# The steps over the row groups written out in full, in place of a loop on the engines

## The reference, cut to what is computed

```
n = layernorm(x)
bias = n @ Wb                                  # (4 heads, 160, 160)
q, k, v = n @ Wq, n @ Wk, n @ Wv               # 160 rows of 160 tokens, 4 heads of 32
attn = softmax(q k^T / sqrt(32) + bias, masked keys at -1e9)
x1 = x + ((attn v) * sigmoid(n @ Wg)) @ Wo
t = layernorm(x1)
p = softmax(t @ router_w + router_b); the best 2 of 8, renormalised
out = x1 + sum over the best 2 of p_e * (t @ expert_w[e] + expert_b[e])
```

## Time and profile before

| | us |
|---|---|
| median of 3 runs | 902.15 (900.57 to 903.08) |
| the profiled execution, its own time | 900.99 |
| span of that execution, first to last instruction | 899.2 |
| PE busy | 818.6 (91%) |
| DVE busy | 778.2 (87%) |
| POOL busy | 645.3 (72%) |
| ACT busy | 501.9 (56%) |

### The profile page before, as it was taken

The page is one execution under the profiler, slowest core; times in us unless marked ns, Lnnn a source line. Parts: engine busy times, 40 slices in busy tenths (PEclk is TensorE's granted clock), DMA queues, the critical chain, the costliest instruction groups (busy, mean ns, idle before and its releaser), DMA issues.

```text
span 899.2 us, 40916 instructions
## 1 busy us (share of the span) xinstructions
PE 818.6 (91%) x15532; PEld 543.4 (60%) x15532; DVE 778.2 (87%) x1818; ACT 501.9 (56%) x1049; POOL 645.3 (72%) x1029
## 2 busy tenths in 40 slices
PE   1999688999999999999999999999999999999643
PEld 1898346666666666666666666666666666666411
DVE  8998445999999999999999999999999999998754
ACT  3886345655655565565655556555565555665310
POOL 6994002587878778787778777777787877888776
PEclk9999999999999999999999999999999999999855
DMA  4563000011111001010010101100010100100000
GB/s 123 193 199 132 30 17 32 25 40 33 47 39 36 29 29 51 29 36 29 29 51 29 36 29 40 41 33 33 29 47 33 36 29 29 51 24 18 24 7 16
DMA packets 32461, 40.82 MB, mean 45 GB/s; under 512 B 6288, under 2 KB 27280, under 8 KB 32400
## 3 DMA queue, kind: packets, MB, share of 16 engines
q1 hardware_dynamic: 31920, 39.95, 13.6%
q10 hardware_dynamic: 480, 0.02, 0.0%
HBM read 13.74 MB, written 6.55 MB: 23 GB/s over the span
## 4 chain that ended last, share of the span: by engine, by line
PE 71%; POOL 10%; DVE 9%; issue 8%; ACT 1%; DVEq 0%; DMA 0%; POOLq 0%; ACTq 0%
PE psS L1117 12%; PE psS L1092 7%; PE psS L1124 5%; PE ps_r L1148 3%; POOL ln_s L375 3%; PE ps_o L1174 3%; PE ps_m L1174 2%; PE psS L1136 2%; PE ps_o L1177 2%; PE ps_m L1177 2%; PE psS L1097 2%; POOL xn L378 2%; PE ps_o L1008 2%; DVE prod L943 2%; POOL add L428 1%
## 5 line engine op out<-in xcount | busy, mean ns | idle before, releaser
L825 DVE TENSOR_REDUCE negm<-psS 128x12 f16<-128x1920 f32 x80 | 145.3, 1816 | 19.5 <-PE psS L1102 17.7
L428 POOL TENSOR_TENSOR add<-prod 128x256 f32<-128x256 f32 x160 | 116.1, 726 | 1.0 <-DVE prod L943 0.9
L433 POOL TENSOR_TENSOR add<-add 128x128 f32<-128x128 f32 x200 | 91.2, 456 | 5.0 <-issue 0.2
L375 POOL TENSOR_TENSOR ln_s<-ln_s,half 128x5 f32<-128x5 f32 (+1 forms) x60 | 86.2, 1437 | 8.0 <-DVE ln_s L737 7.3
L545 ACT ACTIVATE pt_a<-psS 128x1280 f32<-128x1280 f32 x40 | 49.5, 1238 | 71.1 <-PE psS L1126 71.1
L416 POOL TENSOR_TENSOR og_lo<-og,og_hi 128x320 f16<-128x320 f32 x80 | 63.3, 793 | 32.5 <-ACT og_hi L582 32.5
L394 POOL TENSOR_TENSOR xc<-x,ln_s 128x320 f32<-128x320 f32 x40 | 28.9, 722 | 79.0 <-DVE ln_s L874 79.0
L545 ACT ACTIVATE pt_b<-psS 128x1920 f32<-128x1920 f32 x40 | 70.8, 1771 | 17.0 <-PE psS L1136 16.9
L1117 PE MATMUL psS<-bt_hi,ident 128*128 128x320 f16 (+1 forms) x320 | 67.8, 334 | 8.7 <-issue 5.5
L435 POOL TENSOR_TENSOR ymix<-add 128x64 f32<-128x64 f32 x200 | 64.3, 321 | 15.7
L1092 PE MATMUL psS<-bm,ident 128*128 128x480 f16 (+1 forms) x320 | 68.4, 337 | 1.2 <-ACT pt_a L545 1.1
(11 more groups left out here) (287 smaller groups left out, 2950.4 us busy)
## 6 DMA issues: line engine op xcount, KB each, us to landing
xin<-in_x SPq DMA_DIRECT2D x20, 320.0 KB, 2.9
xs_all<-xs_pair SPq DMA_DIRECT2D x20, 320.0 KB, 2.5
xs_q<-xs_all SPq DMA_DIRECT2D x40, 160.0 KB, 2.1
xs_v<-xs_all SPq DMA_DIRECT2D x40, 160.0 KB, 2.1
xin<-in_x SPq DMA_DIRECT2D x40, 160.0 KB, 2.2
out<-res SPq DMA_DIRECT2D x40, 160.0 KB, 1.8
w_raw<-in_expert_w SPq DMA_DIRECT2D x2, 128.0 KB
eb_raw<-in_expert_b SPq DMA_DIRECT2D x15, 2.0 KB
```

The lines of the kernel that those rows point to most:

```text
L375: pool.tensor_tensor(ln_s[a][:, 3, 0:w], ln_s[a][:, 2, 0:w], half[:, 0:w], ALU.pow).then_inc(own, 1)
L428: pool.tensor_tensor(add1[t % 2][:], prod_of(t)[:, 0:4, :], prod_of(t)[:, 4:8, :], ALU.add).then_inc(mix_step[t], 1)
L433: pool.tensor_tensor(add2[t % 2][:], add1[t % 2][:, 0:2, :], add1[t % 2][:, 2:4, :], ALU.add).then_inc(mix_step[t], 1)
L825: dve.tensor_reduce(negm[c][:, :, 0:slots], psS[:, :, 0:slots * N].rearrange("i h (s j) -> i h s j", s=slots), AX.X, ALU.max, negate=True) ...
```

## The change

`run_steps` no longer calls `pairs_loop`: all 46 steps, -2 to 43, are written out on all five engines, with n as a plain number. PE's table of who frees which PSUM bank, which had to be set by hand at the entry of the loop body and behind it, is no longer set, since the written-out order gives the same entries. `N_CONST` becomes 23, so the wait at L753 is for all 23 constants in place of 22, and the one at L880 for 25 in place of 24. The order of the work within a step is untouched on every engine. The loops of the first stage stay.

```
-        N_MEMSET, N_CONST = 18, 22
+        N_MEMSET, N_CONST = 18, 23
...
-        FIRST, LOOP, LOOP_END, LAST = -2, 7, GROUPS - 3, GROUPS + 4
+        FIRST, LAST = -2, GROUPS + 4

         def run_steps(eng, step):

-            for n in range(FIRST, LOOP):
-                step(n, n % 2)
-            pairs_loop(eng, step, LOOP, LOOP_END)
-            for n in range(LOOP_END, LAST):
+            for n in range(FIRST, LAST):
                 step(n, n % 2)
...
             def step(n, a):
                 b = 1 - a
-                if not isinstance(n, int) or n == LOOP_END:
-
-                    last[id(psS)] = max_done[1], n + 1
-                    last[id(ps_r)] = qkl_done[1][1], n + 2
-                    last[id(ps_m)] = prod_done[3], n - 3
-                    last[id(ps_o)] = lg_done, n - 2
-                    last[id(ps_x)] = qkl_done[0][1], n + 2
                 if on(n): scores(n, a, 0)
```

## The result

The changed kernel takes 888.47 us (median of 4 runs, 887.98 to 888.70) against 901.5 us for the kernel before in the same comparison (4 runs, 900.57 to 903.08). The ratio is 0.9854, with a 95% interval of 0.9843 to 0.9866: faster by 1.46%. The forecast was 888.8.

The account below looks back on a forecast made before the run. PE was taken as the bound, losing 0.90 us per loop pass to branches, late `am` and register instructions; 31 written-out steps of 18.13 give 562.03 against 575.38, so 902.15 - 13.35 = 888.8 us, range 886.4 to 893.0.

Parts of the forecast that it names:

- N_CONST: The waits for constants: one increment more, issued by POOL right behind the one waited for before; effect forecast as nothing.
- Written-out steps take 18.13 and stay there: Steps 6 to 36 would each take 18.13 us, as written-out steps 4 and 5: 562.03 against 575.38, 13.35 saved.
- The total: Whole kernel: median 902.15 less 13.35 gives 888.8 us; chance of the forecast 0.80.
- PE's branch is worth its gap: Rival: of the loop's cost only PE's 0.38 us gap per return is saved, 15 x 0.38 = 5.7, 896.5; chance 0.04.
- The DVE's branch reaches PE by way of POOL: In the even step DVE's branch delays POOL's `coef` and `xn`, then DVE's copy and `am`; PE's turn_max starts 0.41 us later.
- The branches of ACT, POOL and SP cost nothing: Loop branches on these three engines, with SP's address registers, cost nothing of their own, being covered by PE's and DVE's work.
- The list that is fetched all the way costs under 1 us: PE's longer instruction list: some 80 more blocks fetched, below 1 us on the path in all, contained in the 18.13.
- The DVE's gap stays at L949 and is free: DVE's 0.28 to 0.30 us gap, taken as its own fetch, stays at the same line (L952 before) and costs nothing.
- the rival's price: Rival: DVE's fetch gap lands between L927 and L833 every second step, 15 x 0.28 = 4.2 us back, 893.0; chance 0.09.
- The tail: The stretch from 824.05 us on, 75.15 long, moves forward as a whole; 1 us allowed either way for the clock.
- The 108 ns for a compare-and-branch: Rule beside the forecast: PE's branch by the skill's figure worth 15 x 0.108 = 1.6 us, time 900.5; trace preferred.

## Why the prediction was right, point by point

- **Written-out steps take 18.13 and stay there: right.** This carried the forecast. 562.03 was forecast for steps 6 to 36, and 562.80 came. The missing 0.8 is six steps of 18.22 or 18.23 and one of 18.38. The last is a gap of 0.27 on POOL ahead of `kept`, once in 31 steps. It stands in step 15 of all six kernels in which POOL's 46 steps are written out behind a looped first stage, and is missing there in those in which POOL is looped or the first stage is written out too. So it belongs to a place in POOL's list, as the DVE's does in its own. What makes the 0.09 of the six was not settled. In five of them it is there long before `am`: the second group of L1114 starts 8.81 and not 8.73 after the opening. There is none with `am` first in the changed kernel, but step 4 of the kernel before with `am` first has it (18.22), so the order of `am` and the copy is not the cause.
- **The total**: the agreement to 0.3 us is in part chance. The forecast took off 13.35 from 902.15; the medians of the comparison differ by 13.03, from 901.5, and the spans of the two traces by 12.4.
- **PE's branch is worth its gap: right.** 15 x 0.38 was 5.7. PE returns 14 times, not 15, and the loop on PE alone costs 4.93 in gaps of 0.33 to 0.38.
- **The DVE's branch reaches PE by way of POOL "at nearly its full size": right for the kernel before, wrong as a rule.** The prediction reasoned that POOL, without slack, passes the delay on. POOL does pass it on: with the loop on DVE alone `coef` and `xn` are as late as that. But this kernel costs only 2.05 us in the stretch. It takes POOL's loop beside it, which puts `xn` 0.07 us ahead of the copy, to make it 7.17. What was missed is that the copy is held only if `xn` is clearly ahead of it, by 0.03 us or more in these traces. The Trainium skill (SBUF — State Buffer, Terms) says that DVE and GpSimd share a port pair that one of them holds for a full instruction while the other is blocked; the ends of the copy and of `am`, 0.02 to 0.07 us behind POOL's instruction in every kernel here in which POOL's started first, agree.
- **The branches of ACT, POOL and SP cost nothing: nearly.** Alone they cost 0.99 us in the stretch. But 4 of the 12.6 us, 7.17 - 2.05 - 0.99, come about only when POOL's list has the loop as well as DVE's (the 0.99 holds ACT and SP too), so "nothing of their own" hid a part that they have in common.
- **The list that is fetched all the way costs under 1 us, contained in the 18.13: right.** PE is idle 0.9 us in 562.8 with 84 blocks more in the whole execution.
- **The DVE's gap stays at L949 and is free: right**, in all 18 even steps. Moved to `coef` it costs 4.43, against 4.2 in the rival's price.
- **`N_CONST`**: not tried alone. Step 0 opens at 106.7 to 107.0 us in the three traces with the old value, and at 106.2 to 107.3 in those with the new one and the same first stage, so no effect can be told.
- **The tail**: 0.83 us shorter, within the 1 us allowed.
- **The 108 ns for a compare-and-branch** in the Trainium skill (Advanced Engine Details and Errata, Control Flow Timing) would have given an estimated 900.5. The trace's 0.38 was the better guide, and the loop on PE alone, with 0.35 per return (4.93 over 14), bears it out.

## What to carry to other kernels

Where a loop's prologue and epilogue are the same steps written out, the trace already holds the answer: compare the full steps outside the loop with those inside. A branch costs where it stands ahead of something that an engine without slack waits for, and costs of two engines' lists do not add up when they decide which of two instructions starts first, so take the loop away from engines in pairs as well as singly before giving a price to each. A loop body should stay below what the engine keeps of its list: here a PE body twice as long turned a return of 0.9 us (12.58 over 14) into one of 6.4.

## What the runs showed of the hardware that I had not expected

- A copy of 128 x 80 elements on DVE took 0.19 or 0.71 us according to whether a POOL instruction started 0.01 us or 0.07 us ahead of it. The time that it is held stands in its length, not in the idle time ahead of it.
- A return into a PE body of some 12 blocks cost 3.5 to 5.4 us of standing, and then some us at the lower clock; into one of 6 blocks 0.33 to 0.53 us of standing.
- DVE shows a gap of 0.27 to 0.31 us every second step at a fixed place of its list, and 56 instructions of no use ahead of it cost the kernel 0.5% by the stretch and 0.7% by the ratios. Instructions that do nothing useful, far ahead of the place, can move the time by more than many edits.
- The first step of the filling (opening of step 0 to that of step 1) lasted from 16.83 to 19.39 us in these traces, though PE's list there is the same in all. This is the largest part of the spread that the changes do not explain; what decides it stays open.
